# Row maxima of attention: one of every two heads gets its maximum from a difference and one plain product, on half the rows of TensorE

## The reference, cut to what matters

```python
h = embedding[x]
q, k, v = split(layernorm(h) @ W_qkv + b_qkv)          # per head
scores = einsum('bihd,bjhd->bhij', q, k) / sqrt(192)
p = softmax(scores, axis=-1)
h = h + einsum('bhij,bjhd->bihd', p, v) @ W_out + b_out
# then a routed FFN, a ReLU-kernel attention and a second routed FFN
```

## Time and profile before

| | us |
|---|---|
| median of 3 runs | 1805.18 (1803.73 to 1810.18) |
| the profiled execution, its own time | 1795.51 |
| its span, first to last instruction | 1793.9 |
| PE busy / DVE busy / ACT busy / POOL busy | 1596.3 / 1090.1 / 627.6 / 423.1 |

### The profile page before, as it was taken

How to read it: one execution, slowest core, us unless ns; L and a number is a source line. 1 busy time by engine, 2 the same in 40 slices (tenths; PEclk the granted TensorE clock), 3 DMA queues, 4 the chain that set the end, 5 groups by cost and what they waited for, 6 DMA issues and landing times. The chain is left out here.

```text
span 1793.9 us, 28354 instructions
## 1 busy us (share of the span) xinstructions
PE 1596.3 (89%) x8964; PEld 865.2 (48%) x8965; DVE 1090.1 (61%) x2478; ACT 627.6 (35%) x849; POOL 423.1 (24%) x518
## 2 busy tenths in 40 slices
PE   4779999999899999875999947899988989999997
PEld 2422332233233332574566634567775656666664
DVE  5978997899799893356233335565544943333336
ACT  3412666576566668410211102222123112212111
POOL 6650000000000000100455525000000226666650
PEclk9866999999999999885899977999899889999999
DMA  2470222022222200630211112000001401111116
GB/s 78 151 169 1 37 37 36 1 35 35 36 35 36 36 1 1 154 119 16 60 42 39 39 46 64 1 10 19 10 18 51 126 18 51 53 50 53 46 42 216
DMA packets 64847, 92.82 MB, mean 52 GB/s; under 512 B 9905, under 2 KB 50036, under 8 KB 63732
## 3 DMA queue, kind: packets, MB, share of 16 engines
q1 hardware_dynamic: 51520, 65.08, 15.3%
q0 software_dynamic: 12288, 25.18, 4.9%
q10 hardware_dynamic: 960, 1.57, 0.4%
HBM read 61.82 MB, written 29.98 MB: 51 GB/s over the span
## 5 line engine op out<-in xcount | busy, mean ns | idle before, releaser
L553 DVE TENSOR_REDUCE sa_half_max<-psum 128x1 f32<-128x512 f32 x768 | 494.5, 687 | 68.8 <-PE psum L656 50.0
L610 ACT ACTIVATE sa_probs<-psum 128x1024 f32<-128x1024 f32 x384 | 372.3, 1022 | 167.2 <-PE psum L647 165.7
L656 PE MATMUL psum<-k_stack,q_stack 96*128 96x512 bf16 x768 | 285.5, 410 | 19.7 <-DVE sa_half_max L553 9.6
L647 PE MATMUL psum<-q_stack,k_stack 97*128 97x512 bf16 x768 | 231.1, 385 | 6.3 <-ACT sa_probs L610 5.4
L656 PEld LDWEIGHTS psum<-k_stack,q_stack 96*128 96x128 bf16 x768 | 75.0, 98 | 274.7 <-issue 133.2
L679 PE MATMUL psum<-sa_probs,sa_v_ext 128*32 128x512 f32 x1536 | 206.6, 610 | 0.6 <-ACT sa_probs L610 0.6
L1580 PE MATMUL psum<-w_e_up_a,ex_xt 128*128 x448 | 172.5, 528 | 0.0
L1430 ACT ACTIVATE ex_silu<-psum 128x384 f32<-128x384 f32 (+1 forms) x112 | 59.3, 529 | 290.8 <-PE psum L1580 288.3
L1470 DVE COPY ex_to_rows<-slot_rows 128x2 uint32 (+1 forms) x56 | 12.8, 229 | 211.5 <-DMA y_rows<-ex_y,ex_to_rows 117.4
L1596 PE MATMUL psum<-w_e_down,ex_g_t 128*128 x752 | 137.2, 334 | 0.5 <-DVE ex_g_t L1462 0.5
L1596 PEld LDWEIGHTS psum<-w_e_down,ex_g_t 128*128 128x128 f32 x752 | 120.7, 190 | 34.5 <-issue 34.5
(11 more groups left out here) (286 smaller groups left out, 2183.1 us busy)
## 6 DMA issues: line engine op xcount, KB each, us to landing
attn<-y_rows SPq DMA_DIRECT2D x24, 384.0 KB, 4.6
q_stack<-qk_parts SPq DMA_DIRECT2D x66, 128.0 KB, 4.3
k_stack<-qk_parts SPq DMA_DIRECT2D x66, 128.0 KB, 6.6
qk_parts<-qk_split SPq DMA_DIRECT2D x16, 384.0 KB, 3.5
x_tokens<-x SPq DMA_DIRECT2D x16, 384.0 KB, 2.6
qk_parts<-qk_split SPq DMA_DIRECT2D x16, 192.0 KB, 4.4
w_e_down<-e_down SPq DMA_DIRECT2D x1, 3072.0 KB, 32.6
out<-h SPq DMA_DIRECT2D x8, 384.0 KB, 4.0
```

Source lines behind the costliest of these rows:

```text
L553: nc.vector.tensor_reduce(half_max[:, g, hd, qt, half:half + 1], slot, AX.X, ALU.max).then_inc(ring_free[r], 1)
L610: nc.scalar.activation(probs[:, st % 2, 2 * pair:2 * pair + 2, :], ps[:, 2 * pair:2 * pair + 2, :], ACT.Exp, scale=SCALE0).then_inc(exp_do ...
L647: last = nc.tensor.matmul(ps[:, hd, :], kst[:, g, hd, kt * P:(kt + 1) * P], qst[:, g, hd, half * HALF:(half + 1) * HALF], start=True, stop ...
L656: last = nc.tensor.matmul(ps[:, 4 + r, :], qst[0:SK, g, hd, qt * P:(qt + 1) * P], kst[0:SK, g, hd, half * 512:(half + 1) * 512], start=Tru ...
```

## The change

The key positions of a head are halved: near (0 to 255 and 512 to 767) and far (the rest). For even heads, a "difference" unit multiplies q by (near key minus far key) into a ring slot, and ACT writes its ReLU to SBUF (`ahead`, a new wait on DVE's use of that buffer); a "both" unit multiplies q by the far keys into another slot, and one DVE instruction (`tensor_tensor_reduce`) adds the two and takes the maximum over the 512, which is the maximum over 1024. Odd heads keep two max units. The products for maxima use 64 rows (four of the six copies) instead of 96: even heads lie in partitions 0 to 63, odd heads' stacks are stored from partition 64 on, so the units of a step go to PE as two pairs, each an even head's product on the lower half of the rows followed by an odd head's on the upper half. The order becomes pair, four scores, pair, outputs.

For this POOL splits the key differences into two bf16 parts in the projection (three more instructions a chunk), SP sends six DMAs a chunk instead of four, and ACT's overwriting waits for these too. The loads of group 0 move from ACT's end into SP's projection stage. A stack is loaded in 28 DMAs instead of 12, a row of maxima in two instead of one, and POOL sets two blocks of unused rows to zero and two rows to 1 at the start of the attention.

```diff
+def load_stack(eng, s, b, g, which, odd):
+    stack, order = ((s.q_stack, Q_STACK), (s.k_stack, K_STACK))[which]
+    for k, part in enumerate(order):
+        row = (DB + k * HD) % P if odd else k * HD
+        src = s.qk_parts[which, part, bass.ds(b * D + g * GD, GD), :].rearrange("(s u r) t -> u r s t", u=2, r=HD)
+        eng.dma_start(stack[row:row + HD, g, odd::2, :], src[odd]).then_inc(s.loaded[g], 16)
+STACK_LOADS = 4 * len(Q_STACK) + DB // HD
...
+            def take_apart(u, k, link):
+                pool.wait_ge(two["sent"][u], START + 16 * SENDS * k)
+                near, far = full[:, u, 1:3, 0:CHUNK // 2], full[:, u, 1:3, CHUNK // 2:CHUNK]
+                high, middle = (differences[:, u, :, part, :] for part in range(2))
+                link(nc.gpsimd.tensor_tensor(apart[:], near, far, ALU.subtract))
+                link(nc.gpsimd.tensor_copy(high, apart[:]))
+                nc.gpsimd.tensor_tensor(middle, apart[:], high, ALU.subtract).then_inc(two["apart"][u], 1)
+                pool.wait_ge(two["apart"][u], START + k + 1)
...
                     sp.wait_ge(two["low"][u], START + 3 * (b + 1))
+                    sp.wait_ge(two["apart"][u], START + b + 1)
...
+                        sp.dma_start(dst.rearrange("c r t -> r c t"), differences[src, u, r]).then_inc(two["sent"][u], 16)
+                    if 0 <= early < 4:
+                        load_stack(sp, s, 0, 0, early // 2, early % 2)
...
-                    act.wait_ge(two["sent"][u], START + 64 * k)
+                    act.wait_ge(two["sent"][u], START + 16 * SENDS * k)
+                    act.wait_ge(two["apart"][u], START + k)
...
-            return [("max", g, k // (2 * TB), k // 2 % TB, k % 2) for k in range(first, last)]
+                odd, half, qt, hd = k % 2, k // 2 % 2, k // 4 % TB, k // (4 * TB) * 2
+                units.append(("max", g, hd + 1, qt, half) if odd else
+                             ("both" if half else "difference", g, hd, qt, half))
...
+            nc.gpsimd.memset(qst[MAX_ODD:DB, :, 1::2, :], 0.0).then_inc(v_init, 1)
+            nc.gpsimd.memset(kst[MAX_ODD:DB, :, 1::2, :], 0.0).then_inc(v_init, 1)
...
+                if kind == "both":
+                    dve.wait_ge(ring_free[r_near], START + k_near + 1)
+                    dve.nop(nofuse=True)
+                    nc.vector.tensor_tensor_reduce(ahead_of[:, u], slot, ahead_of[:, u], 1.0, LOWEST, ALU.add, ALU.max,
+                                                   half_max[:, g, hd, qt, 0:1]).then_inc(ring_free[r], 1)
...
+            def ahead(r, k, u, r_taken, k_taken):
+                act.wait_ge(ring_full[r], START + k + 1)
+                act.wait_ge(ring_free[r_taken], START + k_taken + 1)
+                nc.scalar.activation(ahead_of[:, u], ps[:, 4 + r, :], ACT.Relu).then_inc(ring_free[r], 1)
...
                         exps(b, g, st)
+                        for unit in step_units(g, st, last)[0]:
+                            if unit[0] == "difference":
+                                ahead_in_turn(b, place[last][unit], last)
...
-                    last = nc.tensor.matmul(ps[:, 4 + r, :], qst[0:SK, g, hd, qt * P:(qt + 1) * P],
-                                            kst[0:SK, g, hd, half * 512:(half + 1) * 512], start=True, stop=True)
+                    rows = max_rows_of(hd % 2)
+                    last = nc.tensor.matmul(ps[:, 4 + r, :], qst[rows, g, hd, qt * P:(qt + 1) * P],
+                                            kst[rows, g, hd, half * 512:(half + 1) * 512], start=True, stop=True)
...
-            ORDER = ("scores", "maxima", "scores", "maxima", "maxima", "outputs", "maxima")
+            ORDER = ("maxima", "scores", "scores", "maxima", "outputs")
```

More of the change, by code:

```diff
@@ L44 @@
 K_STACK = (0, 1, 0, 1, 2, 0)
+SENDS = 6
 SK = len(Q_STACK) * HD
+MAX_ODD = SK - DB
+LOWEST = -3.0e38
 M_FEAT = 64
@@ L226, in _ @@
             s.semaphores.make_ready(sp)
-            with sp.Fori(0, B) as b:
+            for b in range(B):
                 for u in range(2):
                     sp.wait_ge(two["low"][u], START + 3 * (b + 1))
+                    sp.wait_ge(two["apart"][u], START + b + 1)
                     cols = slice(u * CHUNK, (u + 1) * CHUNK)
@@ L326, in step @@
                     copy_xt(*nxt)
[L327 to L332, removed]
+            pipeline(act, B, start, step, lambda: None)
         @block.tensor
@@ L460, in softmax_attention, with differences_of @@
         place = {last: {u: n for n, u in enumerate(order(last))} for last in (False, True)}
+        AHEAD_UNITS = [n for n, u in enumerate(before) if u[0] == "difference"]
+        def differences_of(last):
+            return [n for n, u in enumerate(order(last)) if u[0] == "difference"]
+        buffer_of = {last: {n: (len(AHEAD_UNITS) + i) % 2 for i, n in enumerate(differences_of(last))}
+                     for last in (False, True)}
+        PER_TURN = len(differences_of(False))
+        assert PER_TURN % 2 == 0
         def turns(eng, body):
@@ L475, in load_max @@
             sp.wait_ge(max_stored[g], START + 16 * (b + 1))
-            sp.dma_start(qst[SK:SK + 1, g, :, :].rearrange("o s t -> o (s t)"),
-                         max_dram[g].rearrange("(o k) t -> o (k t)", o=1)).then_inc(max_loaded[g], 16)
+            rows = max_dram[g].rearrange("(o s u k) t -> u o s (k t)", o=1, u=2, k=TB)
+            for odd, row in enumerate((SK, MAX_ODD)):
+                sp.dma_start(qst[row:row + 1, g, odd::2, :], rows[odd]).then_inc(max_loaded[g], 16)
         @block.sync
@@ L593, in sequence @@
                         dve.wait_ge(max_stored[unit[1]], START + 16 * (b + 1 if unit[1] == 0 else b))
-                    consume(b, n, unit, r, k)
+                    if unit[0] == "both":
+                        near = place[last][("difference",) + unit[1:4] + (0,)]
+                        consume(b, n, unit, r, k, uses(b, near), buffer_of[last][near])
+                    else:
+                        consume(b, n, unit, r, k)
             turns(dve, sequence)
@@ L646, in scores @@
                 for hd in (2 * pair, 2 * pair + 1):
-                    last = nc.tensor.matmul(ps[:, hd, :], kst[:, g, hd, kt * P:(kt + 1) * P],
-                                            qst[:, g, hd, half * HALF:(half + 1) * HALF], start=True, stop=True)
+                    rows = score_rows_of(hd % 2)
+                    last = nc.tensor.matmul(ps[:, hd, :], kst[rows, g, hd, kt * P:(kt + 1) * P],
+                                            qst[rows, g, hd, half * HALF:(half + 1) * HALF], start=True, stop=True)
                 last.then_inc(scores_done[g], 1)
@@ L653, in produce @@
                 pe.wait_ge(ring_free[r], START + k)
-                if kind == "max":
+                if kind in ("difference", "both"):
+                    hd, qt, _ = unit[2:]
+                    rows = max_rows_of(0)
+                    slot, keys = ps[:, 4 + r, :], s.d_stack[rows, g, hd // 2, :]
+                    if kind == "both":
+                        slot = slot.rearrange("p (c j) -> p c j", c=2)
+                        keys = kst[rows, g, hd, :].rearrange("p (c f j) -> p c f j", c=2, f=2)[:, :, 1, :]
+                    last = nc.tensor.matmul(slot, qst[rows, g, hd, qt * P:(qt + 1) * P], keys, start=True, stop=True)
+                elif kind == "max":
                     hd, qt, half = unit[2:]
-                    last = nc.tensor.matmul(ps[:, 4 + r, :], qst[0:SK, g, hd, qt * P:(qt + 1) * P],
-                                            kst[0:SK, g, hd, half * 512:(half + 1) * 512], start=True, stop=True)
+                    rows = max_rows_of(hd % 2)
+                    last = nc.tensor.matmul(ps[:, 4 + r, :], qst[rows, g, hd, qt * P:(qt + 1) * P],
+                                            kst[rows, g, hd, half * 512:(half + 1) * 512], start=True, stop=True)
                 elif kind == "rows":
@@ L683, in _ @@
             for n, unit in enumerate(before):
-                if unit[0] == "max" and unit[2:] == (0, 0, 0):
+                if unit[0] == "difference" and unit[2:] == (0, 0, 0):
                     pe.wait_ge(loaded[unit[1]], START + 16 * LOADS)
```

115 lines of the change are left out of this document (85 added, 30 removed).

## The result

The changed kernel takes 1781.81 us (median), the kernel before, on the same chip, 1806.28: a ratio of 0.9857 (95% interval 0.9828 to 0.9886). One of the four executions was slow (1830.95 us, granted clock 0.845 against 0.91); the ratio is of the other three, whose median is 1779.95. Predicted were 1773 us, range 1752 to 1832. The medians differ by 24.5 us, the two profiled executions by 11.9 (spans 1793.9 and 1782.0), because before's lay 10.8 us under its median and this one 1.9 over.

The account below looks back on a forecast made before the run. PE was taken to bound the steps and DVE the 84 units ahead. Steps -36, units ahead -8 and projection +12 gave -32 us from a median of 1805.2: 1773 us, range 1752 to 1832.

Parts of the forecast that it names:

- PE in a step: Attention step on PE: scores 0.86, pairs 0.43, outputs 0.99, three more shape changes 0.30, together 2.58 us, 0.25 less.
- rivals of emptying: PE in a step: each change of shape empties PE, 0.164 us each, step 2.80, total 1804 us; chance 0.12.
- serial pairs: PE in a step: a pair's two products run one after the other, step 3.01, total 1840 us; chance 0.09.
- ACT level with PE, 2.62 a step from both: Attention step: ACT's work rises to 2.60 us, the engines sometimes wait for each other, 2.62 a step, 36 us gained.
- ReLU: ACT in a step: the added 128x512 ReLU out of PSUM takes 0.587 us, like a copy, and loads no table.
- Fused instruction: DVE in a step: the add-and-maximum takes 0.69 us, like an add; high bound 1.37.
- The free time: DVE in a step: 0.82 us before the next odd max unit wants the slot; any excess lengthens each step.
- PE waiting on DVE's slots in every step: Attention steps: a sign that would show the forecast wrong.
- Units ahead: The 84 max units before the first step, paced by DVE: 21 x 0.39, 8 us gained (4 to 11).
- Projection: Stage before attention: POOL's added pieces and two more sends a chunk lose 12 us, floor 4, ceiling 20.
- exceeds the 10.34 of a chunk by 1.6: Projection: POOL needs 11.9 us a chunk while there are gathers, four to five chunks, about 7 us lost.
- Earlier loads gain nothing: Projection's end: loading group 0 earlier gains nothing, since the attention's start hangs on SP's last sends.

## Why the prediction was right, and where it was off

- *PE in a step*: right. Predicted 2.58 by its own sum, measured 2.61 to 2.62: pairs 0.215, each change of shape 0.10. The rivals of emptying (0.164 a change) and of serial pairs did not happen; the price of the second was right (3.01 for the step, 3.03 with both heads on the same rows).
- *ACT level with PE, 2.62 a step from both*: the size was right, the reason half wrong. Cutting ACT's part left the median step at 2.62; PE sets it, and the 2.58 lacked 0.04.
- *ReLU*: 0.60 us, no load beside it; 0.59 was taken.
- *Fused instruction*: 0.69 as taken. The free time was given as 0.82 and was 0.70 by the same account: the second product was read 0.57 us after its start (302.67 to 303.24) and not 0.42, which leaves 0.76 to 304.00, and the signal takes 0.06. The doubled instruction (0.61 + 0.69 = 1.30) so has 0.60 too much, and the step grew by 0.61, to 3.23, where the sum gave 3.13 at 1.37. That 0.69 still fitted into 0.70 is luck: PE waiting on DVE's slots in every step was named as a sign of being wrong, and it was 0.01 us away.
- *Units ahead*: -5.7 instead of -8. DVE's busy time fell by 8.7 us (51.1 to 42.4) where 21 x 0.50 = 10.5 were summed: the fused instruction brings a second one of 0.08 us, 1.7 us in all (21 x 0.08). Its idle time rose by 3.0 (2.5 to 5.5) where 21 x 0.1 = 2.1 were allowed for refilled slots.
- *Projection*: the term that was mis-sized, +23.0 against +12 and above its ceiling of 20; the first max matmul came at 132.5 us, and 119 to 125 had been named as a sign of being right. ACT's first write of the sixth chunk came 10.7 us later than before, where the step "exceeds the 10.34 of a chunk by 1.6" gave 7: POOL's whole chunk took 12.4, 2.1 more, and 2.5 us are the later rise of the clock in the first chunk (in the version with half a ReLU this write is 8.4 us late, the first max matmul comes at 130.0 and the loss is 20.4). The last two chunks, counted at nothing, cost 7 more; there DVE was held up by POOL and PE was at its lower clock, and no run takes the two apart. The end cost 5, near the 4.6 said. "Earlier loads gain nothing" was right but not all: they stood in SP's queue before the last sends (125.96 ready, 127.06 sent).
- The median came within 9 us of the forecast, and that is in part luck: the stages that it speaks of gave only -18 of the -32, and the profiled execution, for which the same sum gave 1763.5 us, took 1783.66. The medians lie 24.5 us apart, some 6 more than these stages explain, and that much is within the spread of the untouched rest.

## What to carry to other kernels

Look for the part of a change that carries its gain and leave the rest out: here two halves of TensorE's rows did it alone. Freeing DVE brought nothing in a step that PE sets; in the units ahead, where DVE was the bound, it brought 6 us, of which the later start took back 4 to 5. An extra instruction on an engine that serves a pipeline costs what that engine's rest does not cover, in every turn (3.5 us of pieces made POOL's chunk 2.1 us longer), and it can hold up its neighbour besides. Before splitting work for all data, ask which units will need it: the 84 ahead needed two chunks of eight. And when a stage's start moves by 2 to 3 us, look first whether another execution of the same code moves as much.

## What the hardware showed that I had not expected

- A bf16 matmul on rows 0 to 63 and one on rows 64 to 127 start 0.00 to 0.01 us apart and cost 0.215 us together; each change between such a pair and full rows or 32 columns costs 0.10 us (0.32 = 0.215 + 0.10; serial, 0.54 = 2 x 0.215 + 0.11).
- The fused add-and-maximum on DVE needs a second instruction of 0.08 us that reads its accumulator; in a row of instructions it hides in the first one's tail (0.61 from start to start).
- DVE instructions of 0.17 us took 0.9 to 1.0 us, ending with POOL's. Beside memsets a two-operand one took 0.16 us; a one-operand one lasted 3.3 to 4.1 us beside three of POOL's subtractions in a row.
- PE, fully busy, ran 28 us at 1.2 GHz after a loop turn in one version (5.6 us a step), where the change was back at full clock after 5 us of work (320.77 to 325.47).
